# A cross-attention and expert layer: the bias of v added by TensorE, two VectorE steps moved to ScalarE, and a new order of the queues

## What is computed

```python
d = layernorm(x)
q, k, v = d @ Wq.T + bq, ctx @ Wk.T + bk, ctx @ Wv.T + bv
attn = softmax(einsum('bhqd,bhkd->bhqk', q, k)); v = where(isnan(v), 0, v)
z = einsum('bhqk,bhkd->bhqd', attn, v)
x = x + layernorm(z + d) * gamma + beta
w = top2(softmax(layernorm2(x) @ rW + rb)), normalised
x = x + sum_e w_e * (gelu(zn @ W1[e] + b1[e]) @ W2[e] + b2[e])
```

## Time and profile before

| | us |
|---|---|
| median of 3 runs (lowest, highest) | 878.26 (876.82, 878.76) |
| the profiled execution | 875.23 |
| its span, first to last instruction | 873.4 |
| TensorE busy, share of the span | 751.5, 86% |
| VectorE busy | 671.9, 77% |
| ScalarE busy | 534.7, 61% |
| GpSimd busy | 560.0, 64% |

### The profile page before, as it was taken

One profiled execution on the slowest core, in us unless ns is written; L12 is line 12 of the kernel. 1 busy time (PEld: TensorE's weight loads), 2 busy tenths in 40 slices (PEclk: granted clock), 3 DMA queues, 4 the chain that ended last, 5 costly groups with the idle time before them and its releaser, 6 DMA issues.

```text
span 873.4 us, 26128 instructions
## 1 busy us (share of the span) xinstructions
PE 751.5 (86%) x8056; PEld 584.9 (67%) x8057; DVE 671.9 (77%) x1855; ACT 534.7 (61%) x1412; POOL 560.0 (64%) x611
## 2 busy tenths in 40 slices
PE   3389999999999999999999988538786889999970
PEld 1256677777777777777777655427676779998960
DVE  7389999999999999999999977883468755555630
ACT  3246787888878888888887864425444345554520
POOL 6323877777777787777778754343755567777840
PEclk9699999999999999999999988757999999999995
DMA  8755576676776767758677687512342244443327
GB/s 198 141 131 121 129 166 151 161 172 149 175 163 148 180 152 165 173 139 188 138 176 164 154 247 204 142 34 43 60 60 43 45 67 68 67 61 57 64 36 150
DMA packets 154502, 110.95 MB, mean 127 GB/s; under 512 B 68688, under 2 KB 147884, under 8 KB 153920
## 3 DMA queue, kind: packets, MB, share of 16 engines
q1 hardware_dynamic: 132598, 77.01, 38.9%
q0 software_dynamic: 12192, 19.43, 13.5%
q10 hardware_dynamic: 9658, 13.85, 5.1%
HBM read 39.90 MB, written 23.88 MB: 73 GB/s over the span
## 4 chain that ended last, share of the span: by engine, by line
PE 62%; DVE 14%; issue 7%; DMA 5%; DVEq 4%; POOL 4%; ACT 1%; ACTq 1%; POOLq 0%; SPq 0%
PE pj L866 9%; PE pj L835 9%; PE s_row L880 9%; PE zt L911 8%; PE s_t L899 8%; PE s_row L970 5%; DVE negmax L1344 3%; PE pj L853 3%; PE zt L981 2%; PE pj L981 2%; DMA q_stack<-q_part 2%; DVE v_neg L1446 1%; DVEq L1441 1%; DVEq L1433 1%; PE tr L935 1%
## 5 line engine op out<-in xcount | busy, mean ns | idle before, releaser
L1344 DVE TENSOR_REDUCE negmax<-s_row 100x1 f32<-100x361 f32 x512 | 251.5, 524 | 25.9 <-PE s_row L880 18.9
L1163 ACT ACTIVATE p_t<-s_t 128x400 f32<-128x400 f32 x384 | 188.7, 501 | 61.7 <-PE s_t L899 55.4
L880 PE MATMUL s_row<-stack_x,q_stack 125*128 125x361 bf16 x512 | 133.2, 323 | 14.5 <-DMA q_stack<-q_part 7.9
L899 PE MATMUL s_t<-q_stack,stack_x 128*128 128x100 bf16 x1536 | 129.6, 212 | 14.7 <-ACT p_t L1163 10.5
L899 PEld LDWEIGHTS s_t<-q_stack,stack_x 128*128 128x128 bf16 x1536 | 93.6, 100 | 61.8 <-issue 27.0
L970 PE MATMUL s_row<-w_qkv,v_aug 128*128 128x128 f32 x912 | 115.6, 281 | 15.4 <-DVE v_aug L1435 15.4
L970 PEld LDWEIGHTS s_row<-w_qkv,v_aug 128*128 128x128 f32 x912 | 109.5, 197 | 18.4 <-DVE v_aug L1435 16.5
L866 PE MATMUL pj<-w_qkv,ct 128*128 128x256 f32 x384 | 107.4, 403 | 0.0
L835 PE MATMUL pj<-ct,w_qkv 128*128 128x361 f32 x256 | 94.9, 494 | 10.3 <-DMA bk_s<-in_bk 9.2
L1149 ACT ACTIVATE w_qkv<-s_row,b_k 128x128 f32<-128x128 f32 x228 | 64.9, 368 | 62.5 <-PE s_row L970 62.5
L1349 DVE TENSOR_SCALAR p_t<-p_t 128x1200 f32<-128x1200 f32 x128 | 100.9, 789 | 0.3 <-ACT p_t L1163 0.2
(11 more groups left out here) (234 smaller groups left out, 1482.1 us busy)
## 6 DMA issues: line engine op xcount, KB each, us to landing
stack_x<-k_part SPq DMA_DIRECT2D x192, 192.0 KB, 3.8
q_stack<-q_part SPq DMA_DIRECT2D x186, 64.0 KB, 2.0
ct<-in_ctx_t SPq DMA_DIRECT2D x32, 361.0 KB, 5.0
stack_x<-in_w ACTq DMA_DIRECT2D x8, 512.0 KB, 6.4
w_s<-in_w ACTq DMA_DIRECT2D x14, 256.0 KB, 3.1
zscr<-zn SPq DMA_DIRECT2D x32, 100.0 KB
z_in<-zscr SPq DMA_DIRECT2D x32, 100.0 KB
zf_d<-zf_s SPq DMA_DIRECT2D x32, 100.0 KB
```

The lines of the kernel that those rows point to most:

```text
L880: nc.tensor.matmul(s_row[h % 2][:, 0:KEYS], q_stack[0:MROW, b.slot, h, :], k_stack[0:MROW, b.slot, h, 0:KEYS], start=True, stop=True).then ...
L899: last = nc.tensor.matmul(s_t[g % 2][:, j * Q:j * Q + Q], k_stack[:, b.slot, h, kt * 128:kt * 128 + 128], q_stack[:, b.slot, h, 0:Q], star ...
L1163: nc.scalar.activation(p_t[:, quad % 2, kt, :], s_t[g % 2][:, 0:4 * Q], ACT.Exp).then_inc(exp_done, 1)
L1344: v.tensor_reduce(negmax[:, b.slot, h:h + 1], s_row[h % 2][0:Q, 0:KEYS], AXIS.X, ALU.max, negate=True).then_inc(max_done, 1)
```

## The change

- v's bias: bv_part has bv as a sum of three bf16 parts in rows 0, 32 and 64 (of 96), pick_part is 1 in these rows and 0 elsewhere. A bf16 matmul of the two opens each of the three accumulations of v; project_values then adds the projection.
- ScalarE moves v01 and v2 out of PSUM (values_copied). VectorE's values_biased is gone. VectorE makes the parts once, at the start (bias_parts).
- ScalarE multiplies a tile by its gate (gated, between affine and gelu); VectorE's multiply is gone.
- Places: rows 2, 2, 3, 0, 2, 2, 1, 2, 2; v0 and v1 in slot 1, v2 in the slot before the iteration; most steps of ScalarE, VectorE, GpSimd and SyncE moved; a table each for the last three batches; routing and first tiles anew. The old first gathers stood at slot 388, the new at 393; the old TILE_PLACE had every second slot from 393.

```diff
-TAIL_FROM = B - 2
+TAIL_FROM = B - 3
...
-bv_s = sb(att, "bv_s", [128, D])
+bv_part = sb(att, "bv_part", [96, D], BF16)
+pick_part = sb(att, "pick_part", [96, 128], BF16)
...
+pick_ready, bv_step = sem("pick_ready"), sem("bv_step")
...
-    sp.dma_start(bv_s[:], bv.unsqueeze(0).broadcast_to([128, D])).then_inc(v_const, 16)
+    sp.dma_start(bv_rest, bv.unsqueeze(0).broadcast_to([96, D])).then_inc(v_const, 16)
...
     def project_values(b, kt):
         if b.known and b.index == 0:
...
+            pe.wait_ge(bv_step, BV_STEPS)
...
         bank = pj[1 - kt // 2]
+        nc.tensor.matmul(bank[:, kt % 2 * D:kt % 2 * D + D], pick_part[:], bv_part[:], start=True, stop=False)
         for c in range(2):
             last = nc.tensor.matmul(bank[:, kt % 2 * D:kt % 2 * D + D], ct[:, b.slot, c, kt * 128:kt * 128 + 128],
-                                    wv_s[:, c, :], start=(c == 0), stop=(c == 1))
+                                    wv_s[:, c, :], start=False, stop=(c == 1))
...
+    def gated(k):
+        act.wait_ge(y_biased, k.index + 1)
+        act.wait_ge(gate_ready, 2 * k.index + 2)
+        nc.scalar.activation(ys[:, k.slot], ys[:, k.slot], ACT.Copy, scale=gate[:, k.ring:k.ring + 1]).then_inc(y_ready, 1)
...
+        if not k.known or k.index >= 1:
+            gated(k.later(-1))
...
+    def values_copied(b, last):
+        after(act, v_ready, b.index)
+        if last:
+            act.wait_ge(v2_done, b.index + 1)
+            nc.scalar.activation(v_raw[:, 2 * H:3 * H, :].rearrange("p h d -> p (h d)"), pj[0][:, 0:D], ACT.Copy).then_inc(v2_copied, 1)
+        else:
+            act.wait_ge(v01_done, b.index + 1)
+            nc.scalar.activation(v_raw[:, 0:2 * H, :].rearrange("p h d -> p (h d)"), pj[1][:, :], ACT.Copy).then_inc(v01_copied, 1)
...
+            for b in due(turn, i, s, 1, "ACT", "v2"):
+                values_copied(b, True)
+            for b in due(turn, i, s, 1, "ACT", "v01"):
+                values_copied(b, False)
...
+    gated(Tile(0, NT - 1))
...
-    def values_biased(b, last):
-        after(dve, v_ready, b.index)
-        if last:
-            dve.wait_ge(v2_done, b.index + 1)
-            v.tensor_tensor(v_raw[:, 2 * H:3 * H, :].rearrange("p h d -> p (h d)"), pj[0][:, 0:D],
-                            bv_s[:, :], ALU.add).then_inc(v2_biased, 1)
-        else:
-            dve.wait_ge(v01_done, b.index + 1)
-            bias2 = bv_s[:, :].unsqueeze(1).broadcast_to([128, 2, D])
-            v.tensor_tensor(v_raw[:, 0:2 * H, :].rearrange("p (t h) d -> p t (h d)", t=2), pj[1][:, :].rearrange("p (t n) -> p t n", t=2),
-                            bias2, ALU.add).then_inc(v01_biased, 1)
+    def bias_parts():
+        v.memset(pick_part[:], 0.0).then_inc(pick_ready, 1)
...
+        for r in (0, 32, 64):
+            v.memset(pick_part[r:r + 1], 1.0).then_inc(bv_step, 1)
+        dve.wait_ge(v_const, 32)
...
+        step(v.tensor_copy(bv_part[:], bv_rest))
+        step(v.tensor_tensor(bv_rest, bv_rest, bv_part[:], ALU.subtract))
+        for r in (32, 64):
+            step(v.tensor_copy(bv_part[r:r + 32], bv_rest[r:r + 32]))
+        step(v.tensor_tensor(bv_rest[64:96], bv_rest[64:96], bv_part[64:96], ALU.subtract))
+        step(v.tensor_copy(bv_part[64:96], bv_rest[64:96]))
...
-        dve.wait_ge(y_biased, k.index + 1)
-        v.tensor_scalar(ys[:, k.slot], ys[:, k.slot], gate[:, k.ring:k.ring + 1], None, ALU.mult).then_inc(y_ready, 1)
...
+                bias_parts()
...
+            for b in due(turn, i, s, 1, "DVE", "v_aug"):
+                values_merged(b)
...
-            for b in due(turn, i, s, 1, "DVE", "v01"):
-                values_biased(b, False)
...
-            for b in due(turn, i, s, 1, "DVE", "v_aug"):
-                values_merged(b)
-            for b in due(turn, i, s, 1, "DVE", "v2"):
-                values_biased(b, True)
...
-ROW_COUNTS = (2, 2, 2, 0, 2, 2, 2, 2, 2, 0, 0, 0)
-PE_PLACE = {"v0": 1, "v1": 2, "v2": 0, "k0": 5, "k1": 10, "dt": 2, "q": 6, "z": 7, "zft": 3, "router": 6, "max": 12}
-ACT_PLACE = {"drow": 1, "k0": 6, "k1": 11, "dt": 3, "q": 8, "q_mid": 9, "k_mid": 13, "zt": 5, "zft": 4, "td": 5, "u": 6, "y": 14, "max": 11, "m_high": 8, "m_mid": 10}
-DVE_PLACE = {"stats": 4, "var": 5, "stats2": 9, "var2": 12, "v2": 0, "v01": 1, "v": 9, "logits": 6, "z": 7, "v_aug": 9}
-POOL_PLACE = {"u": 2, "k_low": 13, "rstd": 3, "y": 4, "q_low": 10, "rstd2": 13, "t": 13, "k_rest": 12, "q_rest": 6, "m_rest": 9, "m_low": 11, "xb": 3}
-SP_PLACE = {"zf": 1, "ctx": 5, "q": 10, "k": 11, "zout": 3, "max": 6, "zin": 10}
+ROW_COUNTS = (2, 2, 3, 0, 2, 2, 1, 2, 2, 0, 0, 0)
+PE_PLACE = {"v0": 1, "v1": 1, "v2": -1, "k0": 5, "k1": 10, "dt": 2, "q": 6, "z": 7, "zft": 4, "router": 6, "max": 12}
+ACT_PLACE = {"drow": 1, "k0": 5, "k1": 11, "dt": 4, "q": 8, "q_mid": 9, "k_mid": 13, "zt": 5, "zft": 3, "td": 11, "u": 6, "y": 14, "v2": 0, "v01": 2, "max": 11, "m_high": 8, "m_mid": 10}
+DVE_PLACE = {"stats": 3, "var": 4, "stats2": 8, "var2": 10, "v": 9, "logits": 6, "z": 8, "v_aug": 10}
+POOL_PLACE = {"u": 2, "k_low": 15, "rstd": 4, "y": 6, "q_low": 7, "rstd2": 14, "t": 13, "k_rest": 11, "q_rest": 6, "m_rest": 7, "m_low": 8, "xb": 6}
+SP_PLACE = {"zf": 6, "ctx": 11, "q": 13, "k": 16, "zout": 10, "max": 12, "zin": 12}
...
-ROUTE_PLACE = {"sum_const": 326, "ask0": 369, "exp0": 369, "prob0": 370, "choose00": 372, "choose01": 373, "sum0": 374,
...
-   "gather": 388, "rows": 391, "affine": 391, "tiles": 391, "gelu": 391,
...
-TILE_PLACE = [393 + 2 * k for k in range(NF)]
+ROUTE_PLACE = {"sum_const": 324, "ask0": 368, "exp0": 370, "prob0": 369, "choose00": 370, "choose01": 374, "sum0": 374, "ends0": 377, "places0": 378,
+   "taken0": 378, "split0": 378, "hot00": 379, "hot01": 381, "number00": 380, "number01": 384, "query00": 378, "query01": 384, "lanes00": 382,
...
+   "rows": 393, "affine": 391, "tiles": 392, "gelu": 391, "ask1": 403, "exp1": 403, "prob1": 405, "choose10": 405, "choose11": 408,
...
+   "picks1": 427, "index1": 432}
+TILE_PLACE = [393, 393, 395, 396, 397, 400, 400, 403, 406, 408, 411, 412, 412, 414, 415, 415, 419, 419, 423, 428, 435, 436, 436, 439]
...
-TAIL = {"PE": {"z": 8, "zft": -6, "router": -5}, "ACT": {"td": 8, "u": 2, "y": 5, "zft": -6}, "DVE": {"z": 8, "stats": 0, "var": 1, "stats2": 3, "var2": 4, "logits": -5}, "POOL": {"u": -1, "rstd": 1, "xb": 0, "y": 2, "rstd2": 4}, "SP": {"zout": 8, "zin": 9, "zf": -7}}
...
-START = {"PE": {"k0": 0, "k1": 1}, "ACT": {"k0": 0, "drow": 1, "k1": 1, "dt": 2, "q": 3, "k_mid": 3, "q_mid": 3}, "DVE": {}, "POOL": {"k_rest": 5, "k_low": 7}, "SP": {}}
+TAIL = {29: {'PE': {'z': 8, 'zft': 1, 'router': 2}, 'ACT': {'td': 5, 'u': 5, 'y': 13, 'zft': 1, 'zt': 5}, 'DVE': {'z': 8, 'stats': 2, 'var': 4, 'stats2': 7, 'var2': 10, 'logits': 4}, 'POOL': {'u': 1, 'rstd': 3, 'xb': 4, 'y': 7, 'rstd2': 9}, 'SP': {'zout': 5, 'zin': 8, 'zf': 1}},
+        30: {'PE': {'z': 6, 'zft': -10, 'router': -6}, 'ACT': {'td': 12, 'u': 2, 'y': 3, 'zft': -7, 'zt': 4}, 'DVE': {'z': 8, 'stats': 0, 'var': 1, 'stats2': 3, 'var2': 4, 'logits': -6}, 'POOL': {'u': -1, 'rstd': -1, 'xb': 1, 'y': 5, 'rstd2': 6}, 'SP': {'zout': 9, 'zin': 11, 'zf': -7}},
+        31: {'PE': {'z': 7, 'zft': -7, 'router': -6}, 'ACT': {'td': 8, 'u': 3, 'y': 5, 'zft': -6, 'zt': 5}, 'DVE': {'z': 8, 'stats': 0, 'var': 1, 'stats2': 3, 'var2': 4, 'logits': -6}, 'POOL': {'u': -1, 'rstd': 1, 'xb': -6, 'y': 4, 'rstd2': 4}, 'SP': {'zout': 8, 'zin': 12, 'zf': -11}}}
...
+START = {"PE": {"k0": 1, "k1": 3}, "ACT": {"k0": 2, "drow": 0, "k1": 3, "dt": 0, "q": 4, "k_mid": 9, "q_mid": 4}, "DVE": {}, "POOL": {"k_rest": 13, "k_low": 13}, "SP": {}}
```

## The result

The changed kernel takes 900.92 us (median of 6 runs, 898.70 to 903.78); the kernel before, run on the same chip between them, 876.89 us. It is slower by the ratio 1.0296, 95% interval 1.0269 to 1.0323, some 26 us; the two medians are 24.0 us apart. (One run of the kernel before, beside e9, e11 and e12, took 1840 us in a slow state and is in none of the ratios.) The profiled execution took 903.8 us with a span of 902.0 us, 28.6 us above the span of before.

A forecast was written before the change was run, and what follows sets the result against it. TensorE was taken to bound two of three stages, VectorE mattering only in the hand-over. Middle +28, start 0, hand-over -11 and last tile +0.2 gave +17 us: 894 us, range 867 to 906.

The forecast's parts named there:

- Rows 2, 2, 3: Middle: rows 4 and 6 wait for maxima to free their two PSUM banks, 0.95 us a batch.
- Moving v to ScalarE: Middle: ScalarE takes the copies of v and stays under TensorE in load; worth nothing, late queue 0 to 0.5 us a batch.
- Rival C: Middle: ScalarE's queue is late as well, 0.4 us a batch more, 10 us: 904 us; chance 0.08.
- Bias matmul: Middle, TensorE: three added matmuls a batch cost 0.12 us, bounds 0.12 to 0.33 us a batch.
- rival of a dearer bias matmul: Middle, TensorE: the bias matmuls cost 0.6 us a batch; its chance is not in the text.
- Number of batches: Middle: 26 batches, from 100 to 510 us, pay the new price of 0.95 + 0.12 us, +28 us.
- Start: Start: q's stores leave about 2 us sooner, k's 4 us later; taken at 0, bounds -2 and +4 us.
- Hand-over: From the last batches to the expert tiles: three TensorE gaps shrink, -11 us, bounds -2 and -21.
- Part (3): Hand-over from 640 us: some ten tiles are each 0.37 + 0.08 us shorter on VectorE, -4 us.
- Part (1): Hand-over: the 8.40 us gap before 592.00 goes; tile 0 some 2 us, last batch's z some 9 us earlier.
- A: Whole kernel faster: hand-over gives back more than the middle costs, 4 us in the middle, -15 there, 867 us; chance 0.19.
- D: A rival about TensorE's granted clock, outside the range 867 to 906 us; its exact claim and chance are not in the text.

The follow-up runs named there:

- e9: The changed kernel with GpSimd's subtraction k_rest cut from 722 to 16 elements a row and scores from k's high part alone: 894.56 us, ratio 1.0247.
- e11: The kernel before with only the gate multiply on ScalarE and the new places of last chains, routing and first tiles: 865.65 us, ratio 0.9909.
- e12: As e11, with v's bias as matmuls by TensorE and VectorE moving v out of the banks at the old places: 867.63 us, ratio 0.9927.
- e1: The kernel before with the new row counts 2, 2, 3, 0, 2, 2, 1, 2, 2 alone: 901.48 us, ratio 1.0310.
- e3: The changed kernel with the old row counts 2, 2, 2, 0, 2, 2, 2, 2, 2, all else as changed: 897.85 us, ratio 1.0257.
- e7: The changed kernel without the bias matmul, v's bias left out of the computation: 898.75 us, ratio 1.0280.
- e5: The changed kernel's code with every table of places as in the kernel before: 897.25 us, ratio 1.0274.
- e6: As e5, but with the new places of the last chains, the routing and the first tiles: 892.52 us, ratio 1.0203.
- e13: As e6, with v01 given back to VectorE at its old place and v2 still on ScalarE: 876.94 us, ratio 1.0050.

## Why the prediction was right, and where it was not

**Time.** Forecast 894 us, 867 to 906; measured 900.9. The sum was +17 us on the profiled execution; its two spans differ by 28.6, the medians by 24.0.

**Rows 2, 2, 3 (+0.95 us a batch).** Right as a mechanism and in size: in the changed kernel row 4 starts 0.96 and row 6 1.91 us after row 2, and the two places lose 0.30 + 0.65 = 0.95 of the 1.17 us that the batches 6 to 24 lose in the distances above. The parts alone do not show it as cleanly. In e1 the term is 0.90 us, but with VectorE's bias add in it; undone in the changed kernel (e3) it gives back 0.09, since VectorE's lateness in slots 4 and 5 takes up most of the 0.36 us that are won at its place. That is the step to learn from: a part that gives nothing back when it is undone need not be innocent. The total in the middle, 1.14 against 1.07 us a batch, fits because the term and the bias matmuls are right and what was not foreseen there, the collision and small differences behind slot 4, is about 0.1 us.

**Moving v to ScalarE (0).** In the changed kernel TensorE never waits for v, and the term of 0 stands as far as its waits show. At the old places it is the step that would have failed. I priced the copies well: 0.59 + 0.38 us of ScalarE. I checked that ScalarE stayed under TensorE in load, and put lateness at 0 to 0.5 us with a chance of 0.08. It costs 1.14 us a batch there. The load was not the question. VectorE had been standing idle for v01 (7.2 us before its group from 150 to 460 us, 15.0 over the whole kernel), and ScalarE reaches it behind up to three other steps. Rival C named the queue but asked when the exponentials would be late, not who waits for the bank. What the collision of guard and k_rest costs beside it, 0.16 us in the changed kernel (e9), was in no term. The changed kernel with v given back to VectorE was not tried.

**Bias matmul (+0.12 us a batch, 0.12 to 0.33).** Measured +0.09 in e12 and -0.09 when left out in e7. Three of them take 0.34 us from start to start, and each projection behind one is 0.06 us shorter. Both differences are of one trace each and come to 2.3 us in 25 batches, no more than runs of one kernel differ by; that the matmul is cheap is shown, its exact price is not. The rival of a dearer bias matmul, 0.6 us a batch, is out.

**Number of batches.** I counted 26 at the new price; batches 27 to 31 paid it too, 4.4 us. (In e5 and e6, with as long a period, they did not: 70.3 and 71.3 us.) Start: 0 forecast, +2.3 measured, inside the bounds and inside its scatter over the kernels.

**Hand-over (-11 us).** Measured -7.5 in the tiles and +0.8 ahead of them; in e11 -10.0 and +0.4. Part (3), the gate, is e5's 4.4 us against 4 forecast. Part (1) was half wrong. The gap of 8.40 us did not vanish, it was dealt out. TensorE before the first tile, which starts at 629.82, and its first wait for weights:

```profile
604.73 1.07 PE L925 MATMUL tr<-ident,zt_s 128*100 128x128 f32 x4 [5.30 <-DVE logits L1427]
...
615.10 0.60 PE L932 MATMUL tr<-ident,zf_s 100*128 100x100 f32 x2 [4.43 <-ACT zf_s L1118]
...
625.09 0.59 PE L932 MATMUL tr<-ident,zf_s 100*128 100x100 f32 x2 [6.58 <-ACT zf_s L1118]
...
629.82 0.63 PE L964 MATMUL pj<-ident,q_part 128*128 128x128 f32 x2
...
661.72 3.39 PE L976 MATMUL s_row<-w_qkv,v_aug 128*128 128x128 f32 x16 [2.68 <-DVE v_aug L1470]
```

z of the last batch is now ahead of the first tile, and the tiles run more tightly once begun: the first wait for weights is 2.68 us instead of 4.28, all of them 10.8 instead of 15.4, and the 4.14 us for the last lanes are gone. But the first tile comes no earlier: it starts 44.9 us after the last batch's transpose of the maxima, 44.1 before. What holds it there was not tried.

**Rivals.** A, the gain, fell: the hand-over gave 10 us in e11, not 15. Without the middle's part it is nevertheless what makes e11 faster than before. D fell: the granted clock, in parts of the full one, was 1.00 from 120 to 500 us with rows waiting in every batch. The rule that I had cited from the Trainium skill, "TensorE: Matmul & The Clock Gate", section "A second HAM failure mode: psum-queue depth-cycling", did not act here. One reading under D was wrong: the gap of 4.14 us ends at 681.74, outside the stretch of 640 to 680 us, and right behind it the granted clock of the kernel before fell to the lower level, 1.2 GHz:

```profile
682.00:685.50 3.50, 3.50 (x65) 3.50 (x61) 2.38 (x10) 0.00 (x0) 0.62 (x1) 0.51 0.32 67
```

The gaps that it shows at full clock, before the weights of the tiles from 640 to 680 us, are 1.37 to 2.99 us.

**What was to be seen.** The period rose as forecast, the waits on maxima to 33.6 us (25 or more), the projection behind a bias matmul fell from 1.09 to 1.03 us (0.07). The stretched triple was there: rows 4, 5 and 6 run from 312.59 to 313.86, 1.27 us (1.3), the last behind a wait for a maximum. The pairs ahead of it were stretched as well; that was the sign that something had also come late before the three rows, and it was in the trace of the changed kernel before any experiment. z of batch 31 does stand ahead of the first tile. Tiles 15 and 16 came 5.8 and 7.4 us sooner after the last rows, not 11.

## What to carry to other kernels

Before you move a step that empties a PSUM bank to the engine with the lowest load, read how soon after the producer's end that engine would start it, and who takes the bank next: at the old places here this cost 0.80 us a batch. Where an engine empties two PSUM banks in turn, count the cycle of a bank (0.96 us for two rows here), from the start of a row to the start of its maximum, to its end, to the next row, as the prediction did, and check what else stands in that engine's queue. When a change brings several possible causes, build its parts up from the kernel before as well as undoing them in the one after, and compare the distances of starts at the place that was changed, not the total alone: in e3 a gain of 0.36 us at one place was eaten by 0.25 us at another. And split a mixed change: here its second half alone is worth 1%, and the first half takes it and 3% more.

## What the runs showed of the hardware

VectorE's guard (128x1200 fp32, one operand, SBUF to SBUF) takes 0.77 to 0.79 us in all 79 cases of the kernel before from 150 to 460 us, beside GpSimd steps too. Where it starts while GpSimd's k_rest runs, it took 1.74 to 2.13 us (12 of 73 in the changed kernel): the one that starts at 309.33 ends 0.64 us after k_rest's end at 310.47, and each of the 12 ends 0.64 us after it. Where the guard starts first it is GpSimd that pays, and k_rest ends 1.42 us after the guard's end: 1.56 us if it runs alone, up to 2.16 beside the guard. In the middle of the kernel before the guard always starts first and is nearly done when k_rest starts, so k_rest is at most 0.12 us longer. So the two take turns, and the later one waits; where their starts lie within 0.01 us of each other, either may be the one that waits. In e5 it is k_rest, in e13 the guard:

```profile
302.80 2.21 POOL L768 TENSOR_TENSOR k_rest<-k_rest,k_part 128x722 f32<-128x722 f32 x1 [0.41 <-ACT k_rest L1092]
...
302.81 0.79 DVE L1384 TENSOR_SCALAR p_t<-p_t 128x1200 f32<-128x1200 f32 x1 [0.15 <-DVE st L1409]
```

```profile
296.62 1.56 POOL L768 TENSOR_TENSOR k_rest<-k_rest,k_part 128x722 f32<-128x722 f32 x1 [0.40 <-ACT k_rest L1092]
...
296.63 2.19 DVE L1388 TENSOR_SCALAR p_t<-p_t 128x1200 f32<-128x1200 f32 x1 [0.15 <-DVE st L1413]
```

The Trainium skill, "GPSIMD Engine Reference", section "8. Key points", says that GpSimd shares its SBUF interfaces with VectorE and contends with VectorE's instructions that run in a two-port performance mode or have two SBUF inputs. The trace agrees that these two steps hold each other up; the guard has one SBUF input, and in which mode it runs no trace here shows. The maxima, one input from PSUM, kept 0.52 to 0.53 us on average in all kernels. What the collision cost in time was small (e9), 0.16 us a batch.
